# Banks given out by expected release, and the first normalisation and its two transpositions moved forward in the last slot

## What is computed

```python
def _L0_attn_ref(x, Wq, bq, Wk, bk, Wv, bv, Wo, bo, rw):
    q, k, v = _heads(x, Wq, bq), _heads(x, Wk, bk), _heads(x, Wv, bv)
    qp = jax.nn.relu(jnp.einsum('bhsd,hdf->bhsf', q, rw)) + EPS
    kp = jax.nn.relu(jnp.einsum('bhsd,hdf->bhsf', k, rw)) + EPS
    kv = jnp.einsum('bhsf,bhsd->bhfd', kp, v)
    qkv = jnp.einsum('bhsf,bhfd->bhsd', qp, kv)
    norm = jnp.einsum('bhsf,bhf->bhs', qp, kp.sum(axis=2))
    out = qkv / (norm[..., None] + EPS)
    ...
    return jnp.einsum('bsd,de->bse', out, Wo) + bo
def _L0_ffn_ref(...):
    # router: top 8 of 64 x 64 pairs of keys, for 4 heads, softmax of their scores
    w = jax.nn.silu(w) * jax.nn.softmax(scores, axis=-1)
    experts_states = jnp.einsum('bthk,bthkd->btd', w, ue)
    mlp = jax.nn.silu(hidden_states @ Wg + bg) * (hidden_states @ Wu + bu) @ Wd + bd
    return mlp + experts_states
x = _layernorm(x + _L0_attn_ref(x, ...), axis=-1)
x = _layernorm(x + _L0_ffn_ref(x, ...), axis=-1)
```

## Time and profile before

| | us |
|---|---|
| median of 3 runs | 3829.16 (3826.76 to 3831.45) |
| profiled execution | 3829.62 |
| its span, first to last instruction | 3827.8 |
| PE busy | 3686.1 (96%) |
| DVE busy | 2772.6 (72%) |
| ACT busy | 1914.9 (50%) |
| POOL busy | 1503.9 (39%) |

### The profile page before, as it was taken

How to read it: one execution, slowest core, us unless ns; L and a number is a source line. 1 busy time by engine, 2 the same in 40 slices (tenths; PEclk the granted TensorE clock), 3 DMA queues, 4 the chain that set the end, 5 groups by cost and what they waited for, 6 DMA issues and landing times.

```text
span 3827.8 us, 52117 instructions
## 1 busy us (share of the span) xinstructions
PE 3686.1 (96%) x19388; PEld 3103.1 (81%) x19388; DVE 2772.6 (72%) x5819; ACT 1914.9 (50%) x2502; POOL 1503.9 (39%) x1004
## 2 busy tenths in 40 slices
PE   8979999999999999999999999999999999999988
PEld 7758888888888888888888888888888888777766
DVE  2377777777777777777777777777777777787773
ACT  3345555555555545555554555554555544455441
POOL 0144344334444334444333444433444333444431
PEclk8779999999999999999999999999999999999999
DMA  3000000000000000000000000000000000000000
GB/s 112 17 12 6 15 15 17 17 12 12 17 13 17 17 12 12 17 12 17 18 12 12 17 12 17 17 12 12 18 12 17 17 7 11 12 12 12 6 6 12
DMA packets 23338, 61.16 MB, mean 16 GB/s; under 512 B 5552, under 2 KB 10032, under 8 KB 23088
## 3 DMA queue, kind: packets, MB, share of 16 engines
q1 hardware_dynamic: 18480, 41.04, 3.4%
q0 software_dynamic: 4608, 16.78, 1.1%
HBM read 41.04 MB, written 16.78 MB: 15 GB/s over the span
## 4 chain that ended last, share of the span: by engine, by line
PE 69%; DVE 16%; ACT 6%; issue 6%; POOL 3%; SPq 0%; DMA 0%; DVEq 0%; ACTq 0%; POOLq 0%
PE ring L601 18%; PE y_bank L693 8%; PE y_bank L695 8%; PE step_bank L529 5%; PE step_bank L537 5%; PE step_bank L627 5%; PE step_bank L572 4%; PE step_bank L601 3%; POOL grid L436 3%; DVE prob L1060 3%; PE step_bank L565 3%; PE step_bank L618 3%; PE step_bank L523 2%; PE step_bank L673 2%; ACT grid L826 2%
## 5 line engine op out<-in xcount | busy, mean ns | idle before, releaser
L436 POOL TENSOR_TENSOR grid<-ex 128x1024 f32<-128x1024 f32 x512 | 1054.1, 2066 | 886.3 <-ACT prob L830 309.6
L693 PE MATMUL y_bank<-wd_sb,gate 128*128 128x256 f32 x2048 | 625.9, 388 | 1.8 <-DVE wexp L1082 1.8
L695 PE MATMUL y_bank<-up_sb,wexp 128*128 128x256 f32 x2048 | 612.9, 381 | 0.0
L1047 DVE SCALAR_TENSOR_TENSOR grid<-grid,best 128x1024 f32<-128x1024 f32 x256 | 328.3, 1283 | 296.1 <-POOL grid L436 295.2
L1060 DVE SCALAR_TENSOR_TENSOR prob<-grid,narrow,prob 128x1024 f32<-128x1024 f32 x256 | 466.1, 1821 | 6.9
L601 PE MATMUL ring<-x1T_hl,downT_hl 128*128 128x512 f32 x1536 | 420.6, 410 | 21.9 <-ACT gate L836 21.9
L695 PEld LDWEIGHTS y_bank<-up_sb,wexp 128*128 128x128 f32 x2048 | 392.2, 192 | 54.2
L601 PE MATMUL ring<-x1T_hl,wg_hl 128*128 128x512 f32 x1536 | 425.8, 413 | 3.2 <-DVE gate L1076 3.2
L424 POOL TENSOR_SCALAR qp<-qp 128x512 f32<-128x512 f32 x256 | 265.6, 1038 | 406.9 <-ACT qp L810 399.0
L601 PE MATMUL ring<-x1T_hl,wu_hl 128*128 128x512 f32 x1536 | 418.8, 408 | 0.0
L693 PEld LDWEIGHTS y_bank<-wd_sb,gate 128*128 128x128 f32 x2048 | 356.9, 192 | 44.2 <-issue 15.6
(11 more groups left out here) (151 smaller groups left out, 6304.6 us busy)
## 6 DMA issues: line engine op xcount, KB each, us to landing
xb<-in_L_attn_x SPq DMA_DIRECT2D x34, 512.0 KB, 3.5
out_y<-x POOLq DMA_DIRECT2D x32, 512.0 KB, 3.0
xa<-in_L_attn_x SPq DMA_DIRECT2D x30, 512.0 KB, 3.5
prob<-in_L_ffn_down_embed SPq DMA_DIRECT2D x1, 1024.0 KB, 5.6
prob<-in_L_ffn_Wg SPq DMA_DIRECT2D x1, 1024.0 KB, 8.4
prob<-in_L_ffn_Wu SPq DMA_DIRECT2D x1, 1024.0 KB, 10.8
wd_sb<-in_L_ffn_Wd SPq DMA_DIRECT2D x1, 1024.0 KB, 11.6
up_sb<-in_L_ffn_up_embed SPq DMA_DIRECT2D x1, 1024.0 KB, 12.4
```

The costliest lines, as they stand in the source:

```text
L436: pool.tensor_tensor(grid[:, h % 2], bcast(ex[:, h, 0:NX].unsqueeze(2), [P, NX, NK]), bcast(ex[:, RH + h, 0:NK].unsqueeze(1), [P, NX, NK]) ...
L693: pe.matmul(rows, gate[:, c % 2, t * P:(t + 1) * P], wd_sb[:, c, :], start=(c == 0 and t % 2 == 0), stop=False, skip_group_check=True)
L695: mm = pe.matmul(rows, wexp[:, c % 2, t * P:(t + 1) * P], up_sb[:, c, :], start=False, stop=(c == C - 1), skip_group_check=True)
L1047: marks["keep", h] = rt_steps.mark(dve.scalar_tensor_tensor(out=g, in0=g, scalar=best[:, h, TOP - 1:TOP], in1=g, op0=ALU.is_ge, op1=ALU.mult))
```

## The change

`take` no longer goes round. It keeps an estimated clock of PE's work (`now`, advanced by `WORK` of each step, with entries for the feed-forward work between) and for each bank the time at which it expects it to be read (`held` = end of the step plus `HOLD` of its kind), and gives the bank that is expected free first. `norm1` goes from behind the last `sum` of slot 7 to the head of that slot on DVE, ahead of `ff_h(7)`. On PE both `next` steps go ahead of both halves of `ff_out(7)`. Nothing is added or removed; PE has the same matmuls.

```diff
+        WORK = {"turn": 0.44, "k": 1.73, "q": 1.73, "v": 1.73, "kp": 0.47, "qp": 0.46, "qkv": 1.73, "sum": 1.73,
+                "back": 0.44, "wo": 1.73, "next": 0.44, "rt": 1.39, "pt": 0.44, "ff": 1.39, "out": 1.73}
+        HOLD = {"turn": 2.0, "k": 6.0, "q": 6.0, "v": 4.0, "kp": 2.0, "qp": 2.0, "qkv": 3.5, "sum": 3.0,
+                "back": 2.0, "wo": 3.0, "next": 5.0, "rt": 8.0, "pt": 5.0}
         place, taken = {}, [0] * (STEP_BANKS + 2)
+        now, held = [0.0], [0.0] * (STEP_BANKS + 2)
 
         def take(*use):
             banks = STEP_BANKS + 2 if use[0] == "kv" and use[1] < 2 * FILL else STEP_BANKS
-            k = len(place) % banks
+            kind = use[2] if use[0] in ("kv", "at") else use[0]
+            k = min(range(banks), key=lambda b: held[b])
             place[use] = k, taken[k]
             taken[k] += 1
+            now[0] = max(now[0], held[k]) + WORK[kind]
+            held[k] = now[0] + HOLD[kind]
...
+                    if ff and name in ("ff", "out"):
+                        now[0] += group * WORK[name]
...
                     if ff and c:
                         ff_out(c - 1, 1)
+                    if at:
+                        for use in AT_LATE[c]:
+                            at_use(*use)
                     if ff and c == C - 1:
                         ff_out(c, 0)
-                    if at:
-                        for use in AT_LATE[c][:1]:
-                            at_use(*use)
-                    if ff and c == C - 1:
                         ff_out(c, 1)
-                    if at:
-                        for use in AT_LATE[c][1:]:
-                            at_use(*use)
...
                     uses(AT_EARLY[c])
+                    if at and c == C - 1:
+                        norm1()
                     if ff:
                         ff_h(c)
...
                     uses(KV_LATE[c])
-                    if at and c == 7:
-                        norm1()
```

More of the change, by code:

```diff
@@ L204, in block_kernel @@
             for c in range(C):
-                for name, group, uses in (("kv", it, KV_FIRST[c] if kv else []),
-                                          ("at", it - ATTN_LAG, AT_EARLY[c] if at else []),
+                for name, group, uses in (("kv", it, KV_FIRST[c] if kv else []), ("ff", 1, []),
+                                          ("at", it - ATTN_LAG, AT_EARLY[c] if at else []), ("ff", 1, []),
                                           ("rt", it - ROUTE_LAG, [(c // 2,)] if rt and c % 2 == 0 else []),
-                                          ("kv", it, KV_EARLY[c] if kv else []),
+                                          ("kv", it, KV_EARLY[c] if kv else []), ("ff", 1, []),
                                           ("at", it - ATTN_LAG, AT_MID[c] if at else []),
-                                          ("pt", it - FFN_LAG, [(c,)] if ff else []),
-                                          ("kv", it, KV_LATE[c] if kv else []),
-                                          ("at", it - ATTN_LAG, AT_LATE[c] if at else [])):
+                                          ("pt", it - FFN_LAG, [(c,)] if ff else []), ("out", 1, []),
+                                          ("kv", it, KV_LATE[c] if kv else []), ("out", 1, []),
+                                          ("at", it - ATTN_LAG, AT_LATE[c] if at else []),
+                                          ("out", 2 * (c == C - 1), [])):
+                    if ff and name in ("ff", "out"):
+                        now[0] += group * WORK[name]
                     for use in uses:
```

## The result

| | before | after |
|---|---|---|
| median, us | 3827.96 (3826.61 to 3831.45, 4 runs) | 3795.43 (3789.7 to 3800.0, 4 runs) |
| ratio, 95% interval | | 0.9913 (0.9896 to 0.993) |
| profiled execution, span | 3829.62, 3827.8 | 3796.84, 3795.1 |

A forecast was written before the change was run, and what follows sets the result against it. PE, 96% busy, was taken as the bound, so only its idle time and clock could change. Gains of 39.1 net in full iterations, 21.4 and 3.3 sum to 63.8 us, giving 3765 us; range 3742 to 3792.

The forecast's parts named there:

- The gains of the full iterations: PE's waits at `next` 0 (10.4) and `turn` (26.8 and 14.2) go, plus 8.5 of clock: 59.9 us.
- The new bank wait: PE at `qp` 1 waits for ACT's read of `qp` 0 in the shared bank: 0.80 us in 26 full iterations, 20.8.
- DVE beside POOL's spreads: Iterations 32 to 35: DVE's `lift` took 1.56 beside POOL's spreads, 0.16 elsewhere; `norm1` ends later, 0.6 comes off each gain.
- The rival *Slower: ACT waits for POOL or DVE before its masks, holding `qp` 1; decides from 3.3 us a wait, 3884 at 5.4; chance 0.03.
- The rival of a falling clock: PE's granted clock falls at the new wait at `qp` 1; chance 0.05, outside the range.
- The 1.7 us of a slow stretch: PE's lower clock behind five of the six long `turn` waits costs 1.7 us each, 8.5 in the gains.
- `q` 0 just in time: PE reaches `q` 0 at 1995.05, ACT's copy of `turn` 1 ends 1995.02: no reserve, nothing counted, up to 0.5 us kept.
- Half of the gain moves: Rival: ACT's copy is a little late, `q` 0 waits 0.5 us in 25 iterations; 3790 us, chance 0.16.
- An iteration takes 112.6 us: Sign of being right: a full iteration takes 112.6 us instead of 113.6.
- The table does nothing: Rival: the `qp` 1 wait vanishes and DVE's shift alone would have freed `turn`; 3744 us, chance 0.10.
- Iterations 32 to 35: PE's 3.52 waits at `next` 0 go with their slow clock, less 0.6 each for `norm1` beside spreads: 21.4 us gained.
- Iterations 4 and 5: `k` 1 and `qp` 1 wait for banks, but waits at `next` 0 go: +3.3 us, between -2 and +6.

The follow-up runs named there:

- the kernel with `lift` first: Changed kernel with DVE's small steps reordered to sum, rz, lift, drop, so `lift` precedes `drop`; 3744.92 us, ratio 0.977.
- the other bank: Changed kernel with 4 us more expected hold for `qp` 0, so `qp` 1 gets the bank of `k` 0; 3748.83 us, ratio 0.9785.
- the late `lift`: Changed kernel with one extra unused DVE reciprocal ahead of `rz` in a group's first tile, putting `lift` behind POOL's start; 3839.36 us, ratio 1.0028.

## Why the prediction was wrong

- **The gains of the full iterations** (59.9): right. Without the bank wait they measured 57.3.
- **The new bank wait** (26 x 0.80 = 20.8): place, number and releaser were right, and so was the price in 17 iterations: 0.59 + 0.16 = 0.75 by its rows, 22.4 for all 26 without lost meetings. The step that failed is the sentence that one value holds in every iteration because ACT's queue and PE move together. ACT's queue also waits for DVE's `lift`, and whether that takes 0.16 or 1.91 is decided by some ns. The nine lost meetings cost 25.1 us, nearly all of the 29.3 missing in the full iterations; the rest is 2.6 of gains and 1.6 of this wait. The prediction kept an end of 2.7 us for this wait, but only for another cause, and let none of it into the range.
- **DVE beside POOL's spreads** was weighed for `norm1` alone. In the full iterations each of its instructions took 404 to 410 ns, so none was lengthened there. The `lift` of tile 0, six slots earlier, was not looked at. The prediction calls `lift` "0.16 us elsewhere", and that reading is wrong: the trace of before has 1.52 for it in tiles 1 and 2 of every full iteration, and 1.04 us for `drop` on two numbers, both signs that this chain of DVE is timed by POOL's spreads: in the full iterations the `drop` of tile 0 ends 23 to 27 ns behind the first spread, and the `lift` of tiles 1 and 2 15 to 24 ns behind the second.
- **The rival *Slower*** (0.03) named the wait that came, ACT held by DVE in front of its masks, and was set aside because "in a full iteration ACT has no gap there". That is so in the iteration that was read. In nine of the 26 after the change ACT has a gap of 1.44 there. Its price was another one: it asked for 3.3 us in every iteration, and the wait grew by 1.4 in nine. One of the prediction's signs of being wrong, a wait longer than 1 us at `qp` 1, came true by this, and another, `norm1` well over 1.4 us, in iterations 32 to 35 (below).
- **The rival of a falling clock** was half right. The new wait at its usual length, 0.59, does not bring the lower clock in any of 17 cases. But the wait that grows to 2.00 does, in eight cases of nine, as the waits of 2.2 did before in five of six.
- **The 1.7 us of a slow stretch** (5 x 1.7 = 8.5 in the gains): no run shows them as a time. By the granted clock a stretch is 3.41 us at 0.50, which makes 1.7. As a time, an iteration of the changed kernel with a lost meeting takes 115.75 us from `lift` to `lift` with the stretch and 114.19 without it, which is 1.56 less; there is only one without.
- **`q` 0 just in time**: right. The timeline of PE around iteration 22's start has no wait at `turn` or at `q` 0, nor has any other full iteration a row for them in the view of PE's waits. So the rival *Half of the gain moves* fails by its mechanism; that its time (3790) is near is luck:

```profile
2093.06 0.60 PE L534 MATMUL step_bank<-ident_r,xa 128*128 128x128 f32 x4
2093.60 1.96 PE L540 MATMUL step_bank<-qp,wq_sb 128*128 128x512 f32 x4
```

- **An iteration takes 112.6 us**: nearly. Where no meeting is lost, from `lift` to `lift` it is 852.17 - 739.39 = 112.78:

```profile
739.39 0.16 DVE L1047 TENSOR_TENSOR narrow<-best,narrow 128x2 f32<-128x2 f32 x1
852.17 0.16 DVE L1047 TENSOR_TENSOR narrow<-best,narrow 128x2 f32<-128x2 f32 x1
```

and where one is lost 1080.70 - 964.96 = 115.74.

- **The table does nothing** (0.10): right on the half that matters most. With `norm1` early the wait at `turn` is gone under either table, and the run of the table alone shows that the table removes it as well: either part would have brought the 26.8, and with the moves in place the table adds nothing. The other half, that the wait at `qp` 1 vanishes, is wrong.
- **Iterations 32 to 35** (21.4, measured 17.4): the four waits of 3.5 are gone, but `norm1` now runs beside the spreads of POOL, and took 3.4 us longer. DVE and PE there, and the sum of the waits at `qp`:

```profile
3410.10 1.56 DVE L1047 TENSOR_TENSOR narrow<-best,narrow 128x2 f32<-128x2 f32 x1
3411.58 4.73 DVE L1015 TENSOR_SCALAR x<-x,mv,rstd 128x256 f32<-128x256 f32 x4
...
3348.17 0.73 PE L629 MATMUL step_bank<-qT_hl,rw_hl 128*128 128x512 f32 x2 [2.01 <-ACT qp L817]
3418.91 0.67 PE L704 MATMUL y_bank<-wd_sb,gate 128*128 128x256 f32 x2 [0.42 <-DVE wexp L1089]
...
PE step_bank L629 <- ACT qp L817: 6.4, 4, 2.0
```

`norm1` took 4.73 in place of 1.37. The prediction expected it behind the second spread and let POOL's third come late in its favour; it was the other way round, and beside the third spread the last of the four instructions took 2.09, where the two before it took 0.40 each. PE waits 0.42 for `ff_wexp(7)` behind it. The waits at `qp` are 6.4 in all, and those for ACT's gate fell from 21.9 to 17.0, so most of the first is hidden in the second, as the prediction had it.
- **Iterations 4 and 5** (+3.3, measured 5.5): the sign is as forecast, but the fill varies by up to 4.7 us between kernels with the same work there (281.1 and 276.4), so the size is not shown and the sign hardly. `qp` 1 was held 8.4 us in iteration 5 (the longest in the first row of PE's waits), more than the 5.4 read before.

The measured runs of the changed kernel spread over 10 us. A number of lost meetings that differs from run to run at 2.8 us each would fit, but it is not shown, and the kernel with `lift` first speaks against it as the main cause: it loses none in its profiled execution and spread over 16 us, and the kernel before, which lost none in its profiled execution either, spread over 15 in the same round. Open too is why the meeting was never lost before and was lost nine, six and four times in three of the kernels: the starts of POOL relative to `lift` lie a few ns earlier in them, but so they do with the other bank (2 to 5 ns ahead, none lost), and what shifts them was not found. I also did not try `norm1` at another place in iterations 32 to 35, where it collides with the spreads.

## What to carry to other kernels

A bank should not be given again to the next step of the same kind while its reader has a queue ahead of it: a wait of 0.6 us a round looks cheap, but it can hand a delay of that reader's queue on to the matrix engine (here 44.3 us for 17 delays of ACT's mask, and nothing with another bank). Before you trust a wait to stay as long as its row says, follow the reader's chain back to instructions whose duration jumps (here a `drop` of 1.04 for two numbers), and look at what POOL starts within a tenth of a us of them (here 7 ns). Read such an instruction in all tiles and not in one: `lift` took 0.16 in tiles 0 and 3 and 1.52 in 1 and 2, and the short one was taken for the rule. Of a change with two parts that remove the same wait, measure each alone: here one part gave 2.2%, the other 0.7%, and both together 0.9%.

## What the runs showed of the hardware

- **A difference of nanoseconds decides over 1.75 us.** In the changed kernel, with POOL 7 ns ahead, an instruction of DVE on 128 x 2 numbers took 1.91 us and ended 15 or 16 ns behind POOL's spread of 1.90; with POOL 2 to 6 ns ahead, it took 0.16. In the run of the moves alone both outcomes stand at 5 and at 6 ns. That most short cases also have POOL slightly ahead, and that one and the same distance has both outcomes, shows that the printed starts are not exactly the moments that decide. What decides, no trace shows.
- **Such meetings come back.** DVE's `drop` and POOL's first spread end together (23 to 27 ns apart), from there to the next start it is 0.34 us on DVE and 0.36 on POOL (iteration 12 above), and so DVE's `lift` and POOL's second spread start within 7 ns of each other in all 26 iterations of before and of after. With `lift` ahead of `drop` they don't meet any more: `lift` and `drop` take about 0.60 and 0.15 each time, the second spread starts 0.87 to 0.94 us behind `lift`'s start, and DVE's busy time falls from 2778.4 to 2618.2 us between the two kernels with the moves alone that differ in nothing else.
- **The clock.** In the full iterations no wait of PE of 0.59 was followed by the lower level (17 in the changed kernel, 26 with `lift` first, 22 with the table alone), and none of the 19 of 1.25 before; of the nine of 2.00, eight were, each with 3.41 us at a granted clock of 0.50. It is no fixed rule: five of the six waits of 2.2 before, two of the four of 2.00 with the table alone and 21 of the 25 of 2.0 with the late `lift` were.
